# Layer 3 of a graph network: the scaling of its features moved from GpSimd to ScalarE

## The reference, cut to what matters

```python
ft = (feat @ W.T).reshape(n, HEADS, OUT_DIM)
a1 = jnp.einsum('nhd,hd->nh', ft, attn_l)
a2 = jnp.einsum('nhd,hd->nh', ft, attn_r)
e = jax.nn.leaky_relu(a1[src] + a2[dst], negative_slope=ALPHA)   # ALPHA = 0.2
m = jax.ops.segment_max(e, dst, num_segments=n)
ex = jnp.exp(e - m[dst])
s = jax.ops.segment_sum(ex, dst, num_segments=n)
a = ex / s[dst]
out = jax.ops.segment_sum(ft[src] * a[:, :, None], dst, num_segments=n)
return jax.nn.elu(out)
```

## Time and profile before

| | |
|---|---|
| median of 3 runs | 2018.65 us |
| lowest and highest of them | 2015.79 and 2025.22 us |
| the profiled execution's own time | 2015.71 us |
| its span | 2013.9 us |
| mean granted TensorE clock | 0.904 of full speed |
| first pass of layer 3 | about 1572 to 1630 us from the start of the span |

### The profile page before, as it was taken

The page is one execution under the profiler, slowest core; times in us unless marked ns, Lnnn a source line. Parts: engine busy times, 40 slices in busy tenths (PEclk is TensorE's granted clock), DMA queues, the critical chain, the costliest instruction groups (busy, mean ns, idle before and its releaser), DMA issues. The chain is left out here.

```text
span 2013.9 us, 28671 instructions
## 1 busy us (share of the span) xinstructions
PE 1737.0 (86%) x10386; PEld 1111.1 (55%) x10386; DVE 1245.8 (62%) x1653; ACT 532.9 (26%) x854; POOL 1086.3 (54%) x1646
## 2 busy tenths in 40 slices
PE   5866976879988998898566699999998899999997
PEld 1245752237665675575444476567797454545453
DVE  7875748974434444355222255565656899999995
ACT  2300002005543544444223355240005211111111
POOL 4887888888888888888888881000000610000000
PEclk8855557989999999999777799999998999999998
DMA  9777864004535445354333253209770576766672
GB/s 349 295 292 301 320 263 157 9 2 132 196 121 173 144 150 196 107 187 134 128 122 108 99 197 131 92 29 312 237 235 1 161 249 216 234 214 228 205 230 85
DMA packets 254470, 354.47 MB, mean 176 GB/s; under 512 B 123880, under 2 KB 230045, under 8 KB 247838
## 3 DMA queue, kind: packets, MB, share of 16 engines
q1 hardware_dynamic: 138923, 306.98, 42.7%
q10 hardware_dynamic: 89654, 45.29, 7.6%
q0 software_dynamic: 25792, 0.88, 1.1%
HBM read 221.53 MB, written 131.55 MB: 175 GB/s over the span
## 5 line engine op out<-in xcount | busy, mean ns | idle before, releaser
L415 POOL DMA_INDIRECT table<-valT,idxT x806 | 780.3, 968 | 168.5 <-issue 142.4
L2207 DVE SCALAR_TENSOR_TENSOR wgt<-ratio,l3q,fcj 128x1664 f32<-128x1664 f32 (+1 forms) x195 | 365.9, 1910 | 26.7 <-PE psum L2251 18.2
L2247 PE MATMUL psum<-wgt,big 128*32 128x384 f32 (+1 forms) x3200 | 355.8, 495 | 7.2 <-DVE wgt L2207 7.2
L916 PE MATMUL psum<-hx,region 128*128 128x257 f32 x1250 | 302.9, 388 | 19.5 <-issue 13.6
L916 PE MATMUL psum<-region,g 128*128 128x512 f32 (+1 forms) x672 | 275.4, 555 | 1.1 <-DVE big L694 1.1
L413 POOL MEMSET rest<- 128x256 f32 x805 | 265.1, 329 | 1.0 <-DMA table<-valT,idxT 0.5
L694 DVE TENSOR_TENSOR big<-big,psum 128x512 f32<-128x512 f32 (+1 forms) x325 | 210.2, 665 | 86.3 <-PE psum L916 58.8
L916 PEld LDWEIGHTS psum<-hx,region 128*128 128x128 f32 x1250 | 231.8, 195 | 57.4 <-issue 20.1
L2251 PE MATMUL psum<-wgt,l3e 128*32 128x384 f32 (+1 forms) x1600 | 253.5, 494 | 0.0
L2247 PEld LDWEIGHTS psum<-wgt,big 128*32 128x32 f32 x3200 | 140.3, 110 | 142.9 <-issue 127.3
L916 PEld LDWEIGHTS psum<-region,g 128*128 128x128 f32 x672 | 123.2, 192 | 123.1 <-issue 111.1
(11 more groups left out here) (260 smaller groups left out, 1690.6 us busy)
## 6 DMA issues: line engine op xcount, KB each, us to landing
table<-tk SPq DMA_DIRECT2D x25, 3200.0 KB
tk<-table SPq DMA_DIRECT2D x25, 1664.0 KB
fcj<-counts_b SPq DMA_DIRECT2D x20, 2080.0 KB, 8.6
tk<-table SPq DMA_DIRECT2D x25, 1536.0 KB
fcj<-counts_b SPq DMA_DIRECT2D x19, 1920.0 KB, 8.2
counts_t<-region ACTq DMA_DIRECT2D x25, 800.0 KB
counts_b<-region ACTq DMA_DIRECT2D x25, 800.0 KB
table<-valT,idxT POOLq DMA_INDIRECT x806
```

Of the source, the lines that this page charges most:

```text
L415: eng.indirect_dma_start(out=table, out_offset=bass.IndirectOffsetOnAxis(idxT[:, c:c + 1], 0), in_=valT[:, c, :], in_offset=None).then_inc ...
L916: mm = lambda o, l, r_, st, sp: eng.matmul(o, l, r_, start=st, stop=sp, skip_group_check=True)
L2207: eng.scalar_tensor_tensor(out=tiles_of(wgt[:, n % NW, :]), in0=tiles_of(rb[:, p % 2, :]), scalar=qs[:, k, h:h + 1], in1=cj[:, m % NC, 0:n ...
L2247: eng.matmul(acc[p % 2][at:at + QUARTER, bank, 0:hi - lo], ftx[:, k, h, QUARTER * v:QUARTER * v + QUARTER], wgt[:, (NT * p + k) % NW, lo:h ...
```

## The change

The features of tiles 1 to 24 are scaled on ScalarE. One instruction handles one head of one tile, with the factor as its scale operand, so a tile takes four. VectorE keeps tile 0 alone, since FIRST goes from 3 to 1. GpSimd has nothing left to do in layer 3 but its wait. The row copies, which ScalarE used to do one after another, now stand between scalings: row copy g comes right behind the scaling of tile g+10.

```diff
-        NW, NC, FIRST = 4, 2, 3
+        NW, NC, FIRST = 4, 2, 1
...
         @block.gpsimd
         def _(eng):
             eng.wait_ge(s_("exp"), 2)
-            for k in range(FIRST, NT):
-                eng.tensor_tensor(ftx[:, k, :, 0:HD], ftx[:, k, :, 0:HD], e2[:, k, :].unsqueeze(2).to_broadcast([P, H, HD]), ALU.mult)\
-                   .then_inc(s_("ft"), 1)
...
-            for g in range(7):
+
+            def scaled(k):
+                for h in range(H):
+                    last = eng.activation(ftx[:, k, h, 0:HD], ftx[:, k, h, 0:HD], ACT.Copy, scale=e2[:, k, h:h + 1])
+                last.then_inc(s_("ft"), 1)
+            eng.wait_ge(s_("exp"), 2)
+
+            def take_row(g):
                 w = min(4, NT - 4 * g) * P
                 eng.wait_ge(s_("rowed"), g + 1)
                 eng.activation(rsb[:, 4 * g * P:4 * g * P + w], pR[0:H, g % 2, 0:w], ACT.Copy).then_inc(s_("rows"), 1)
+            for k in range(FIRST, NT):
+                scaled(k)
+                if 0 <= k - ROWS_AT - 4 < 7:
+                    take_row(k - ROWS_AT - 4)
...
-                    if p == 0 and k + 1 < FIRST:
-                        scaled(k + 1)
```

## The result

The changed kernel is slower by a third of a per cent. Over 12 runs each its median is 2024.43 us (2019.03 to 2042.5) against 2016.62 us (2015.13 to 2025.22) before. The ratio is 1.0032, with a 95% interval of 1.0017 to 1.0048. That is about 6.5 us (the plain difference of the two medians is 7.8), less than the 0.5% that the prediction called telling, but clear of zero. The forecast of +0.2 us missed it. The execution at 2042.5 us had a granted clock of 0.87, the other eleven had 0.899 to 0.905; the median hardly feels it.

What follows compares the result with a forecast made beforehand. TensorE was taken to set layer 3's pace. Terms: 0 (GpSimd) + 0 (VectorE) + 0.2 (block 5 beside block 4) + 0 (ScalarE) = +0.2 us, giving 2018.9 us beside the median of 2018.65; range 2012.0 to 2025.4.

Steps and rivals of the forecast that it cites:

- a late ScalarE: Rival, chance 0.06: in layer 3's first pass costlier scalings delay row copies or products, up to 6.8 us lost, 2025.4.
- the four rivals: VectorE deciding (0.09), ScalarE late (0.06), clock and other things (0.05), and fourth the forecast itself, nothing depending on the change (0.80).
- The clock rival: Rival, 0.05 with other things: layer 3's product 1 also runs at half clock, losing another 1.65 us, 2020.6.
- the first term of the sum: Layer 3: GpSimd's 22 scalings go; no product waited for them by more than rounding, so gain 0.
- VectorE faster, and no gain: Layer 3: without GpSimd, weights start 1.73 us apart, not 2.09, but VectorE then waits for TensorE; gain 0.
- The rival that VectorE decides: Rival, chance 0.09: each weight's 0.36 us gain in layer 3 reaches TensorE, 6.8 us in all, 2011.8.
- Block 5 beside block 4: First pass: block 5's load, 0.8 us earlier, may share DMA with block 4 and delay product 20; cost 0 to 0.4, taken 0.2.
- What holds block 4: First pass: SP's row jobs behind the last row copy, not the weights the chain names, hold this load; it stays at 1609.8.
- ScalarE: Layer 3: 96 scalings of about 0.21 us, 0.86 us per tile, fit into ScalarE's free time; cost 0.
- its thresholds, 1.69 and 2.1 us per tile: First pass: at 0.42 us per scaling the last row copy slips; at 0.53 us scalings and copies no longer fit the pass.

Runs made afterwards that it cites:

- e3: The kernel before with GpSimd's 22 scalings taken out and not done elsewhere, so features of tiles 3 to 24 stay unscaled; ratio 1.0034 to the kernel before.
- e1: The changed kernel plus one GpSimd multiply of 128x4 in layer 3, into a buffer nothing reads; ratio 1.0003 to the kernel before.
- e10: The kernel of e1 plus 15 GpSimd memsets of 128x700 ahead of the select at the start; ratio 1.0031 to the kernel before.
- e7: The kernel of e1 with block 4's load issued ahead of the store of the row copies; ratio 0.9999 to the kernel before, layer 3 441.6 us.
- e12: The kernel of e1 with each ScalarE scaling cut in two of 32 columns; layer 3 took 441.5 us, no ratio.
- e8: The kernel of e1 with each ScalarE scaling cut into four of 16 columns; one timed run of 2043.39 us, layer 3 467.2 us.
- e2: The changed kernel plus one GpSimd memset of 128x4 in layer 3, where e1 has its multiply; ratio 1.0037 to the kernel before.
- e11: The kernel of e1 plus 30 GpSimd memsets of 128x700 ahead of the select at the start; ratio 1.0091 to the kernel before.

## Why the prediction was right and wrong

**The range held by luck.** The measured 2024.43 us lies inside 2012.0 to 2025.4, and the change was indeed under 0.5%. But the upper end stood for a late ScalarE, which did not come, and none of the four rivals is what happened. The range was also built on 2018.65 us, the median of three runs; twelve give 2016.62, and with its upper end moved down by the same 2.0 us, to 2023.4, the measured time lies outside. Nor is 0.5% the least that can be told: these runs tell 0.32%, with 0.16% to either side. (The clock rival's 2020.6 was counted from 2018.9, the others from 2018.65; from there it is 2020.3.)

**The step that failed** is the first term of the sum: "GpSimd's 22 instructions go. [...] Gain 0." For layer 3 it holds. As a sum for the kernel it is wrong, because it prices removed instructions only where they stood. By theory A they also left GpSimd set up for the select at the start of the next execution. The term should have been +4.0 to +4.7 us (first scatter, stalled profiles against before), and the ratio says 6.5 us (3.4 to 9.7). That taking the multiplies away is enough is shown (e3), that a multiply of 128x4 restores the time is shown (e1), and that the lateness alone costs this much is shown (e10). That the 11 us are a fetch of code, and that the code stays over from the execution before, is the one reading of e1 to e3 that I know of, and it is not shown. Neither a row nor the DMA queues of the changed kernel between 3.5 and 15 us name a fetch. The record does not say what ran just before each execution; alternating two kernels would separate what the last execution left from what is fixed when a program is built. The rows had a hint beforehand: GpSimd's scalings had 10.1 us of idle time put down to "issue" and began at 1580.8, 7.5 us after their factors. I took the row for its busy time and did not ask what the wait was, nor where it would go when its instruction went. The Trainium skill ("GPSIMD Engine Reference", "2.1 Instruction dispatch") gives about 6 us for the first call of freshly loaded code, with no instruction to show it. The rows agree in kind, with no row for the gap, and have 8.6 and 11.0 us in place of 6; the measured ones count here.

**VectorE faster, and no gain** was right. Its first five weights took 8.73 us, which is (8.73 - 1.82) / 4 = 1.73 us apart, and its wait for TensorE grew by 4.8 us, where I had expected some 6. TensorE's products kept 1.94 us (1616.61 to 1630.18 holds seven). The rival that VectorE decides falls with e3 too.

**Block 5 beside block 4** was put at +0.2 us and cost nothing that shows. Block 4 took from 1620.53 to 1630.54, 10.0 us as before, though block 5 was now free to go at 1618.82 + 7.62 = 1626.44, 5.9 us behind block 4's issue against 6.6 before. The other profiles settle it better than this pair. From the issue of block 4 to the weights that need it, the two of the kernel before have 10.0 and 10.1 us, and the ten in which block 5 was free 5.9 us behind have 9.7 to 10.2, with a mean of 9.9. An even sharing would have added 0.3. So of the bounds, 0 to 0.4, the lower one holds, as if the two loads went one behind the other.

**What holds block 4** was read rightly: SP's row jobs, not the weights in the chain. In the changed kernel the load went out 3.5 us behind the last row copy again, with VectorE ahead, and e7 moved it by moving the queue.

**ScalarE** was mis-sized a little: 0.24 us per scaling and not 0.21 (40 in 9.65 us), so 0.96 us per tile. The last row copy still had 0.73 us of idle time ahead of it, and started 0.11 us behind product 12, as before. The rival's mechanism is borne out, and its thresholds, 1.69 and 2.1 us per tile (0.42 and 0.53 us per scaling), are bracketed. At 8 x 0.21 = 1.7 us per tile (e12) the last row copy has no idle time left and nothing moves yet; at 3.2 us (e8) layer 3 grows by 25.7 us, where the expectation had worked out 26. No run lies between.

**The clock** stayed out of it: product 0 took 3.71 us at a granted clock of 0.51, and 3.59 at 0.50 before. The rival's case did occur in part in one execution, e2's: there product 1 took 2.62 us in place of 1.94, at a granted clock of 0.74, and that layer 3 was the longest but e8's, 442.3 us.

**Still open** is a smaller thing. The changed kernel's ratios (1.0032, 1.0038) and those of e2 and e3 (1.0037, 1.0034) all lie above the 0.20 to 0.23% by which the first scatter is late. The lower ends of the intervals, 1.0017 to 1.0024, reach down to it or nearly. Plain lateness shows an excess too: e10's ratio says 6.3 us where its first scatter is 5.0 late, and e11's 18.4 where it is 16.3. So some 1 to 3 us are not accounted for, and they hardly grow with the lateness.

No version beat the kernel before. With one small GpSimd multiply the scalings on ScalarE cost nothing and bring nothing.

## What to carry to other kernels

When a change removes an engine's last instructions of a kind, ask what state they left behind. Here one multiply near the end of the program decided whether 11 us were lost at its start, most likely the start of the next execution. When the code around a change shows the same length to 0.1 us, stop looking there and compare the traces from their start: the first instruction that is late names the cause. An idle time with no releaser is a question, even off the critical path, since it can move onto it.

## What the runs showed of the hardware

From the setup pair to the first multiply behind the reduction over partitions GpSimd took 8.6 us (kernel before) and 8.8 us (e1). In the kernels whose last instruction with such a pair was the reduction, the select at the start came 10.8 to 11.0 us behind its pair; this lies in idle time that the profile puts down to "issue". Memsets ran without it, in front of the select and in layer 3 (e2). Memsets of 128x700 that each wait for the one before ran 0.73 us apart. A ScalarE copy with a scale from SBUF took 0.24 us per 64 columns, 0.21 per 32 and 0.20 per 16, back to back, so nearly all of it is fixed cost, some 0.19 us by an estimate from the first and last of these.
